# Half of batch 1's recurrence steps placed beside the first feed-forward batch of a decoder layer

## The reference

```python
    def _L0_attn_ref(x, Wqkv, bqkv, Wo, bo):
        kqv = x @ Wqkv + bqkv                       # k, q, v in 16 heads of 32
        scores = jnp.einsum('bsnh,btnh->bnst', k, q) / math.sqrt(HEAD_SIZE)
        scores = jnp.triu(scores) + -10000.0 * jnp.tril(ones, k=-1)
        attn = jax.nn.softmax(scores, axis=2)
        out = jnp.einsum('bnkq,bnkh->bqnh', attn, v)
        return out.reshape(b, s, NUM_HEADS * HEAD_SIZE) @ Wo + bo
...
            def step(carry, kv_t):                  # w, u: one value per feature
                p, q, o = carry
                kt, vt = kv_t
                no = jnp.maximum(o, u + kt)
                A, E = jnp.exp(o - no), jnp.exp(u + kt - no)
                y = (A * p + E * vt) / (A * q + E)
                no2 = jnp.maximum(w + o, kt)
                A2, E2 = jnp.exp(w + o - no2), jnp.exp(kt - no2)
                return ((A2 * p + E2 * vt, A2 * q + E2, no2), y)
...
        g = jnp.einsum('bsh,ih->bsi', hidden_state, Wg)   # W = (integers - 128) * scale
        u = jnp.einsum('bsh,ih->bsi', hidden_state, Wu)
        return jnp.einsum('bsi,hi->bsh', jax.nn.silu(g) * u, Wd)
...
    x = _layernorm(x + _L0_attn_ref(x, ...), axis=-1)
    x = _layernorm(x + _L0_xattn_ref(4, 512, 512, L0_xattn_w, L0_xattn_u, x, ctx_2048), axis=-1)
    x = _layernorm(x + _L0_ffn_ref(x, ...), axis=-1)
```

## Time and profile before

| | us |
|---|---|
| median of 3 runs | 755.16 (754.89 to 755.61) |
| profiled execution, own time | 756.78 |
| its span | 755.0 |

### The profile page before, as it was taken

The page is one execution under the profiler, slowest core; times in us unless marked ns, Lnnn a source line. Parts: engine busy times, 40 slices in busy tenths (PEclk is TensorE's granted clock), DMA queues, the critical chain, the costliest instruction groups (busy, mean ns, idle before and its releaser), DMA issues.

```text
span 755.0 us, 11764 instructions
## 1 busy us (share of the span) xinstructions
PE 712.7 (94%) x4168; PEld 387.6 (51%) x4168; DVE 497.8 (66%) x1165; ACT 427.4 (57%) x1009; POOL 298.7 (40%) x325
## 2 busy tenths in 40 slices
...
GB/s 272 253 99 126 160 206 110 139 127 98 53 61 70 86 115 67 129 96 140 1 1 198 26 0 2 43 15 0 1 15 29 14 1 1 28 29 1 0 15 42
DMA packets 45530, 54.15 MB, mean 72 GB/s; under 512 B 4896, under 2 KB 34848, under 8 KB 45472
## 3 DMA queue, kind: packets, MB, share of 16 engines
...
## 4 chain that ended last, share of the span: by engine, by line
PE 77%; DVE 10%; ACT 5%; issue 4%; POOL 2%; DMA 2%; SPq 1%; POOLq 0%; ACTq 0%; DVEq 0%
PE psb L781 29%; PE psb L794 7%; PE psb L792 7%; PE psb L669 6%; PE psb L707 6%; PE psb L752 5%; PE psb L685 4%; PE psb L720 4%; PE psb L696 3%; DVE ee L1019 2%; PE psb L768 2%; ACT ee L874 2%; PE psb L740 2%; ACT ee L885 1%; DVE ek L1116 1%
## 5 line engine op out<-in xcount | busy, mean ns | idle before, releaser
L1019 DVE CUSTOM_DVE_ANT_0 ee<-psb,mask,clip 128x512 f32<-128x512 f32 (+3 forms) x256 | 130.2, 535 | 28.6 <-PE psb L696 28.4
L874 ACT ACTIVATE ee<-ee,nm 128x512 f32<-128x512 f32 (+3 forms) x256 | 142.6, 559 | 8.4 <-DVE nm L1019 8.2
L1317 POOL TENSOR_TENSOR hl<-hf,hh 128x512 f16<-128x512 f32 x64 | 75.0, 1172 | 119.5 <-ACT hh L950 119.5
L885 ACT ACTIVATE ee<-psb 128x512 f32<-128x512 f32 (+1 forms) x164 | 90.0, 549 | 54.1 <-PE psb L707 42.1
L707 PE MATMUL psb<-ident,ee 128*128 128x128 f32 x640 | 102.2, 276 | 5.3 <-DVE ee L1033 2.8
L950 ACT ACTIVATE hh<-hf 128x512 bf16<-128x512 f32 x64 | 40.3, 630 | 116.0 <-DVE hf L1143 111.4
L1143 DVE SCALAR_TENSOR_TENSOR hf<-th,c,psb 128x512 f32<-128x512 f32 x60 | 44.0, 733 | 88.7 <-PE psb L781 62.1
L781 PE MATMUL psb<-x2h,wg 128*128 128x512 f16 x256 | 97.6, 381 | 0.0
L781 PE MATMUL psb<-x2l,wg 128*128 128x512 f16 x256 | 97.5, 381 | 0.0
L781 PE MATMUL psb<-x2h,wu 128*128 128x512 f16 x256 | 97.0, 379 | 0.0
L781 PE MATMUL psb<-x2l,wu 128*128 128x512 f16 x256 | 97.0, 379 | 0.0
...
## 6 DMA issues: line engine op xcount, KB each, us to landing
...
```

Source lines behind the costliest of these rows:

```text
L874: e.activation(dst, dst, ACT.Exp, bias=NM[:, n % 4, col:col + 1], scale=-1.0, accum_out=DEN[:, n % 4, col:col + 1]).then_inc(sem("exp"), 1)
L885: e.activation(ET[h][:, base:base + width], PSB[:, bank["turn", H, item], 0:width], ACT.Copy).then_inc(sem("et"), 1)
L1019: e.tensor_tensor_reduce(E[H % 3][:, EOFF[i]:EOFF[i] + w], PSB[:, bank["score", H, i], 0:w], MASK[:, S - w:S], -SC, CLIP[:, i:i + 1], ALU. ...
L1317: e.tensor_tensor(HS[it][1][:], ring(b, it)[1][:], HS[it][0][:], ALU.subtract).then_inc(sem("hl"), 1)
```

## The change

Nothing is computed otherwise; the tables of the timetable have other numbers. Steps (1,2) and (1,3) of the recurrence move from slots 209 and 225 to slots 262 and 264, beside hidden units 6 and 8 of batch 0, and with them the transposes of batch 1's result from slots 249 to 255 to slots 268 to 270 and those of its x for the feed-forward part from 265 to 269 to slots 272 to 274. Steps of batches 2 and 3 move by 4 to 11 slots. `KEYS` gives the product of keys and values to VectorE for all batches (before: GpSimd for batches 0 and 1). `COPIES` marks 4 groups of heads instead of 7. All other tables have new numbers. One line is new in `gu_parts`: before unit 0 of a batch, held-back pieces are put into the list until the last `x2l` of this batch is in it.

```diff
-QK_AT = {2: (5, 18), 3: (22, 30), ... 7: (83, 91), ... 14: (194, 199), 15: (218, 220)}
+QK_AT = {2: (5, 17), 3: (21, 26), ... 7: (84, 91), ... 14: (202, 210), 15: (215, 224)}
...
 WAIT = {'high': 1, 'low': 1, 'vtake': 1, 'r1': 1, 'norm': 3, 'exp': 3, 'eb': 1, 't1': 1, 't3': 1, 'oh': 3, 'ol': 3,
-        'ek': 2, 'scan_q': 4, 'scan_p': 4, 'divide': 7, 'r2': 1, 'x2h': 2, 'x2l': 2, 'expand': 0}
-WAIT_IN = {'r1': 0, 'norm': 2, 'ek': 0, 'scan_q': 1, 'scan_p': 4, 'divide': 4, 'r2': 2, 'x2h': 4, 'x2l': 6}
+        'ek': 1, 'scan_q': 2, 'scan_p': 6, 'divide': 7, 'r2': 1, 'x2h': 1, 'x2l': 1, 'expand': 0}
+WAIT_IN = {'r1': 1, 'norm': 0, 'ek': 1, 'scan_q': 1, 'scan_p': 1, 'divide': 2, 'r2': 0, 'x2h': 4, 'x2l': 0}
...
-BO_AT = (19, 111, 131, 181)
-XLOAD = {1: (0, 14, 22, 30), 2: (38, 65, 105, 108), 3: (114, 128, 149, 158)}
-XSPLIT = {1: (29, 32, 34, 37), 2: (89, 100, 105, 105), 3: (157, 160, 163, 171)}
+BO_AT = (5, 104, 120, 182)
+XLOAD = {1: (3, 16, 22, 23), 2: (51, 66, 84, 93), 3: (105, 120, 146, 157)}
+XSPLIT = {1: (29, 29, 35, 35), 2: (91, 99, 107, 107), 3: (156, 161, 162, 167)}
...
-WKV_AT = {(0, 0): 111, (0, 1): 118, (0, 2): 126, (0, 3): 137, (1, 0): 172, (1, 1): 184, (1, 2): 209, (1, 3): 225,
-          (2, 0): 262, (2, 1): 265, (2, 2): 270, (2, 3): 275, (3, 0): 280, (3, 1): 286, (3, 2): 290, (3, 3): 294}
-YT_AT = {0: (155, 155, 157, 167), 1: (249, 252, 252, 255), 2: (280, 280, 283, 284), 3: (299, 299, 299, 300)}
-X2_AT = {0: (223, 229, 229, 233), 1: (265, 268, 268, 269), 2: (289, 289, 291, 293), 3: (305, 305, 306, 307)}
-WO_IN = (10, 11, 13, 15)
-ZERO_IN = (0, 3, 3, 6, 7, 7, 7, 9, 9, 10, 11, 13, 13, 16, 18, 18)
+WKV_AT = {(0, 0): 112, (0, 1): 123, (0, 2): 134, (0, 3): 147, (1, 0): 194, (1, 1): 212, (1, 2): 262, (1, 3): 264,
+          (2, 0): 269, (2, 1): 274, (2, 2): 279, (2, 3): 281, (3, 0): 291, (3, 1): 294, (3, 2): 297, (3, 3): 299}
+YT_AT = {0: (166, 167, 169, 172), 1: (268, 268, 269, 270), 2: (286, 288, 289, 290), 3: (307, 307, 309, 311)}
+X2_AT = {0: (226, 227, 232, 233), 1: (272, 273, 273, 274), 2: (292, 293, 293, 293), 3: (312, 313, 313, 314)}
+WO_IN = (10, 11, 15, 15)
+ZERO_IN = (9, 10, 11, 13, 14, 14, 14, 14, 14, 14, 14, 14, 14, 14, 14, 14)
 
-KEYS = (1, 1, 0, 0)
+KEYS = (0, 0, 0, 0)
 
-COPIES = (1, 0, 1, 0, 0, 0, 1, 0, 0, 0, 1, 0, 1, 1, 0, 1)
+COPIES = (0, 0, 1, 1, 1, 0, 0, 0, 0, 0, 0, 1, 0, 0, 0, 0)
...
             name = "gate" if p < 2 else "up"
+            if it == 0 and p == 0:
+                tt.flush(("x2l", b, T - 1))
             if p % 2 == 0:
```

More of the change, by code:

```diff
@@ L44 @@
 EARLY = 4
-QK_AT = {2: (5, 18), 3: (22, 30), 4: (36, 52), 5: (53, 62), 6: (72, 81), 7: (83, 91), 8: (108, 112), 9: (124, 127),
-         10: (135, 143), 11: (153, 157), 12: (171, 178), 13: (188, 192), 14: (194, 199), 15: (218, 220)}
-V_AT = {1: (41, 44, 56, 69), 2: (114, 126, 127, 135), 3: (178, 184, 186, 194)}
-WO_AT = {0: (89, 98, 100, 108), 1: (141, 145, 147, 151), 2: (200, 208, 212, 226)}
-EARLY_AT = (245, 255)
-FIN_AT = {0: (2, 0, 3), 1: (1, 0, 4), 2: (2, 2, 15), 3: (2, 5, 11), 4: (1, 0, 1), 5: (2, 1, 14), 6: (0, 7, 10),
-          7: (3, 0, 6), 8: (2, 0, 9), 9: (1, 0, 1), 10: (1, 0, 10), 11: (1, 0, 1), 12: (1, 0, 6), 13: (2, 13, 15),
-          14: (0, 2, 14)}
@@ L56 @@
-WAIT = {'high': 1, 'low': 1, 'vtake': 1, 'r1': 1, 'norm': 3, 'exp': 3, 'eb': 1, 't1': 1, 't3': 1, 'oh': 3, 'ol': 3,
-        'ek': 2, 'scan_q': 4, 'scan_p': 4, 'divide': 7, 'r2': 1, 'x2h': 2, 'x2l': 2, 'expand': 0}
-WAIT_IN = {'r1': 0, 'norm': 2, 'ek': 0, 'scan_q': 1, 'scan_p': 4, 'divide': 4, 'r2': 2, 'x2h': 4, 'x2l': 6}
-PIECE_AT = {'load_second': 42, 'small': 62, 'split_wo': 53, 'load_ds': 208}
-WU_AT = (28, 45, 70, 81)
-WU_ZERO = (56, 79, 93, 96)
-WG_AT = (199, 210, 222, 223)
-WG_ZERO = (205, 236, 239, 241)
@@ L64 @@
-REST_AT = (2, 3, 102, 53)
-BO_AT = (19, 111, 131, 181)
-XLOAD = {1: (0, 14, 22, 30), 2: (38, 65, 105, 108), 3: (114, 128, 149, 158)}
-XSPLIT = {1: (29, 32, 34, 37), 2: (89, 100, 105, 105), 3: (157, 160, 163, 171)}
-WKV_AT = {(0, 0): 111, (0, 1): 118, (0, 2): 126, (0, 3): 137, (1, 0): 172, (1, 1): 184, (1, 2): 209, (1, 3): 225,
-          (2, 0): 262, (2, 1): 265, (2, 2): 270, (2, 3): 275, (3, 0): 280, (3, 1): 286, (3, 2): 290, (3, 3): 294}
-YT_AT = {0: (155, 155, 157, 167), 1: (249, 252, 252, 255), 2: (280, 280, 283, 284), 3: (299, 299, 299, 300)}
@@ L73 @@
-X2_AT = {0: (223, 229, 229, 233), 1: (265, 268, 268, 269), 2: (289, 289, 291, 293), 3: (305, 305, 306, 307)}
-WO_IN = (10, 11, 13, 15)
-ZERO_IN = (0, 3, 3, 6, 7, 7, 7, 9, 9, 10, 11, 13, 13, 16, 18, 18)
-KEYS = (1, 1, 0, 0)
-COPIES = (1, 0, 1, 0, 0, 0, 1, 0, 0, 0, 1, 0, 1, 1, 0, 1)
+QK_AT = {2: (5, 17), 3: (21, 26), 4: (37, 39), 5: (53, 61), 6: (67, 82), 7: (84, 91), 8: (109, 111), 9: (122, 128),
+         10: (132, 144), 11: (155, 157), 12: (171, 178), 13: (181, 195), 14: (202, 210), 15: (215, 224)}
```

13 lines of the change are left out of this document (added).

## The result

The changed kernel takes 747.0 us (median of 4 runs, 743.93 to 747.73) against 755.35 (754.89 to 755.61) in the same session: 0.988 of the time, 95% interval 0.985 to 0.991. Forecast was 746.0. The profiled execution took 746.68 us, with a span of 744.9. The profiled execution of the kernel before (756.78) was slower than its median, so the spans differ by 10.1 us and the medians by 8.4.

What follows compares the result with a forecast made beforehand. VectorE was taken to bound three of four attention pieces (168.7 to 369.4 us), TensorE the third and the feed-forward part. -10.0 - 1.8 + 0 + 2.6 = -9.2 from 755.16 gave 746.0 us; forecast 742 to 750, range 739 to 755.

Steps and rivals of the forecast that it cites:

- 1.1 kept back: Four pieces from 168.7 to 369.4 us: 1.1 us of the 11.1 us gain withheld for engines waiting on each other more often.
- VectorE's relief: From 168.7 to 369.4 us: net 12.5 us of VectorE's work leaves, times 0.87 is 10.9 us of its time.
- Groups 7 and 8: First of four attention pieces: VectorE's load 47.4 plus the old addition of 4.7 gives 52.1 us.
- rival (b): More than the sum: 3.2 us of lockouts at the first norm go, first 168.7 us give 2 to 4; 738 to 741; 13 in 100.
- Groups 13 and 14: Fourth attention piece: VectorE's load 40.7 plus the old addition of 3.4 gives 44.1 us.
- The rate: Four attention pieces: 10.9 us less of VectorE's time was to give -10.0 us, each piece lasting its larger load plus something.
- copies, 3.8 us, prices times 0.87: From 168.7 to 369.4 us: VectorE's copies fall from 13 to 4, 9 x 0.42 = 3.8 us; net prices scaled by 0.87.
- Rival (d): Feed-forward part: batch 1's norm is late for its hidden unit 0, despite 6 us of cover; 1 in 100.
- The end of the attention part: From 369.4 to 411 us: batch 1's transposes, residuals and statistics leave, -1.8 us; TensorE's 2.7 us wait for GpSimd's widened row stays.
- Rival (c): Recurrence steps: product and scan one slot behind the exponential make VectorE wait; 758 at 2 us each, 766 at 3.3; 9 in 100.
- Rival (a): Attention part: engines only change places, ScalarE's and TensorE's chains take over; 753.5 to 751 us; 12 in 100.
- The port rule: VectorE and GpSimd lock shared ports in turn; six products locked out at 1.27 us each, 7.6 us, would make 753.6.

## Why the prediction was right, and where it was not

The total was forecast as -9.2 us and came out as -8.2 to the median named there, within the range; its parts did not all come. In spans, in us:

| | forecast | measured | others, same order |
|---|---|---|---|
| groups 0 to 6 | 0 (-5 to +3) | +0.9 | |
| groups 7, 8 | -1.8 | -6.6 | -6.6 |
| groups 9, 10 | -1.2 | +0.2 | -0.1 |
| groups 11, 12 | -4.2 | -4.1 | -4.8 |
| groups 13, 14 | -3.9 | -2.3 | -2.3 |
| 15 to hidden unit 5 | -1.8 | -1.2 | -1.6 |
| from there | +2.6 | +2.9 | |
| sum | -9.2, with 1.1 kept back | -10.2 | |

The last column is read from other kernels, those that have the changed kernel's order in that part and the full clock.

- **VectorE's relief** was sized at 10.9 us and is 18.9 (180.9 less 162.0). The scans are the difference. The prices of 1.52 and 1.56 us are means over the whole program, while the 16 scans of this part took 28.3 us, 1.77 each, and the 12 that are left take 15.2: 13.1 us, where the two steps' prices had 6.2. The norms give 2.1 more (11.7 to 9.6), which the sum had at nothing. Reciprocals (7.4) and copies (3.8) came as priced, and the six products cost 4.5 for 4.1. Why the scans that stay became shorter was not isolated: before, seven of the eight first scans took 1.58 to 2.33 us with a pass of GpSimd beside them, and now all six take 1.22; of the second scans four of eight took 2.2, and now four of six take 1.22 with no pass beside them. The kernel with the old KEYS (16.2 us for its 12) and the one with the steps put back (21.0 for 16) keep most of this. The distances in `WAIT` also changed (`scan_q` 4 to 2, `scan_p` 4 to 6), and no run undoes them alone.
- **Groups 7 and 8** were mis-sized by 4.8 us. 3.7 of it came back with the bias passes' old slots, the first norm's lockout and the scan behind it, which I had put into rival (b) at 3.2 instead of into the sum, though the earlier trace rows showed it and the table of the change moved it. That rival was right in this part; its other part, a gain before 168.7, did not come.
- **Groups 9 and 10**: VectorE's work fell by 1.5 us and the time didn't. The norm of batch 1 takes 3.58 us beside GpSimd in place of 1.91, and undoing that gave 1.25. The forecast weighed each norm's place for the first batch only.
- **Groups 11 and 12**: -4.2 and -4.1 agree, and TensorE is the bound as said; putting its products back shows it.
- **Groups 13 and 14**: I took 44.1 us from VectorE's load over two groups. One group at a time, TensorE is busy for 27.21 of the 27.25 us of group 13, and group 14 lasts 18.49 with TensorE at 14.08. Averaged over two, a full group disappears behind an empty one. The prediction also says that VectorE is the larger load in two of four pieces afterwards; its own figures have three (47.4, 46.0 and 40.7 against 46.2, 40.1 and 38.4), and the profile has one, the second. The larger load of each group, summed over groups 7 to 14, is 192.5 of 200.7 us before and 181.8 of 188.0 after: 10.7 less, against a length 12.7 less.
- **The rate** of 10 us of time for 10.9 of VectorE's did not hold: 18.9 us of VectorE's went with 12.7 of time in the four pieces, 0.67 for each. The time came out only because the relief was larger than sized. By kind it is 0.15 to 0.3 for the reciprocals (0.8 to 1.6 of 5.4), 0.63 for whole steps in the old order, 1.0 and 0.8 for steps in the new one, and 2.6 in the run with the copies (6.9 of 2.7), where ScalarE's work moved too. That it counts whether a mask pass or a bank of TensorE stands behind the instruction fits these and is not shown by itself.
- **The step "copies, 3.8 us, prices times 0.87"** failed: undoing the whole list cost 6 us in the new order. The sum over all pieces hid this.
- **Feed-forward**: 24 transposes, 2.6 us forecast, 2.9 measured; no wait of TensorE. Rival (d), a late norm of batch 1, is out.
- **The end of the attention part**: TensorE's wait for the widened row stayed, 2.8 us, as said; -1.2 to -1.6 came for -1.8.
- **Rival (c)**, waits for the exponential: out. In the attention part there are 1.1 us in three times, and the 16.1 of the feed-forward part hide behind TensorE.
- **Rival (a)**, the engines change places and 751 to 753.5 us come out: out by its number. Taken by single groups VectorE was the busier one only in groups 7, 10 and 14 before (26.9 against TensorE's 24.7 us in group 7), and of these only group 7 changed (20.3 against 21.9).
- **The port rule** for the six products: 753.6 did not come, but this says nothing against the rule, and the argument made against it in the prediction did not test it. Five of the six products have no pass of GpSimd beside them but a clearing of one column (0.10 us), and so it is with the eight of the earlier trace rows. The sixth began while GpSimd was at work and is the long one:

```profile
192.79 1.05 DVE L1100 TENSOR_TENSOR ekv<-ek,ct 128x512 f32<-128x512 f32 x1
...
192.13 1.16 POOL L1267 TENSOR_TENSOR ol<-eb,oh 128x512 f16<-128x512 f32 x1
```

It ended 0.55 us after that pass. Three products in the feed-forward part met one too and took 0.97 to 0.98 us. What the sum by the rule had wrong is how often a product meets a pass. The norms agree with the rule: 5.16, 4.59 and 3.58 us with GpSimd's passes beside, 1.91 without.

The time thus came out right by luck as well: groups 7 and 8 gave 4.8 us more than forecast, and the other parts together 4.9 less (0.9, 1.4, 0.1, 1.6, 0.6 and 0.3), so that the spans' sum is the forecast without the 1.1 kept back. That the moved steps make room and that the rest of the change needs it was right and is shown in both orders.
